# Two gathers at a time: when a graph-attention kernel refills the slots of its ring

## The reference: what is computed

```
h = (x @ W).reshape(n, heads, out_ch)
a_src = sum(h * att_src, -1);  a_dst = sum(h * att_dst, -1)
e = leaky_relu(a_src[src] + a_dst[dst], 0.2)
p = exp(e - segment_max(e, dst)[dst])
alpha = p / segment_sum(p, dst)[dst]
out = segment_sum(h[src] * alpha[..., None], dst)
```

## Time and profile before

| | |
|---|---|
| three runs | 3718.09, 3707.99, 3710.98 us; median 3710.98 us |
| the profiled execution: its own time, its span | 3708.69 us, 3706.9 us |
| busy: PE, DVE, POOL, ACT | 2639.1, 2394.2, 1820.5, 1181.5 us |
| gathers of walk 1, of walk 2 (POOL) | 880 each, 854.8 and 840.7 us busy |
| granted TensorE clock, 300 to 1500 us and 1800 to 3100 us | 0.91 and 0.75 |

### The profile page before, as it was taken

One profiled execution on the slowest core, in us unless ns is written; L12 is line 12 of the kernel. 1 busy time (PEld: TensorE's weight loads), 2 busy tenths in 40 slices (PEclk: granted clock), 3 DMA queues, 4 the chain that ended last, 5 costly groups with the idle time before them and its releaser, 6 DMA issues. The chain is left out here.

```text
span 3706.9 us, 57874 instructions
## 1 busy us (share of the span) xinstructions
PE 2639.1 (71%) x11245; PEld 1963.1 (53%) x11246; DVE 2394.2 (65%) x7306; ACT 1181.5 (32%) x4644; POOL 1820.5 (49%) x1892
## 2 busy tenths in 40 slices
PE   8577777777777777794666666556666666599998
PEld 6455555555555555573455444444444434566666
DVE  6778777777777778884555545555655666635445
ACT  5533433333333333341222111122222211342332
POOL 0365666566656656304555556666655564501111
PEclk9799998889999898997777777777776776599999
DMA  5466666666666666413444563633333333422220
GB/s 192 148 188 187 192 188 193 185 185 189 188 188 185 188 190 184 122 52 114 139 138 135 136 177 106 181 106 106 102 95 95 96 108 103 138 75 64 68 89 12
DMA packets 230811, 511.90 MB, mean 138 GB/s; under 512 B 49249, under 2 KB 116044, under 8 KB 230611
## 3 DMA queue, kind: packets, MB, share of 16 engines
q0 software_dynamic: 118128, 361.70, 34.6%
q1 hardware_dynamic: 97958, 134.64, 12.0%
q10 hardware_dynamic: 14524, 13.40, 1.1%
HBM read 463.94 MB, written 49.57 MB: 139 GB/s over the span
## 5 line engine op out<-in xcount | busy, mean ns | idle before, releaser
L1329 POOL DMA_INDIRECT weights<-table,w_idx x880 | 840.7, 955 | 718.9 <-issue 313.4
L815 POOL DMA_INDIRECT w_G<-table,w_idx x880 | 854.8, 971 | 605.5 <-issue 299.2
L927 PE MATMUL PS<-w_G,w_S 128*128 128x260 f32 x3520 | 954.4, 428 | 90.9 <-DVE ACC L1016 57.7
L927 PEld LDWEIGHTS PS<-w_G,w_S 128*128 128x128 f32 x3520 | 724.1, 212 | 253.8 <-issue 99.9
L1515 PE MATMUL PS<-weights 128*128 128x257 f32 x1760 | 618.9, 497 | 119.3 <-issue 55.5
L1515 PEld LDWEIGHTS PS<-weights 128*128 128x128 f32 x1760 | 398.9, 247 | 227.8 <-issue 135.7
L1004 DVE TENSOR_TENSOR w_G<-w_G,PS 128x512 f32<-128x512 f32 x660 | 432.3, 683 | 68.2 <-ACT PS L838 31.2
L1710 DVE TENSOR_TENSOR ACC<-ACC,PS 128x257 f32 x464 | 196.3, 423 | 412.1 <-remote 185.7
L1016 DVE TENSOR_TENSOR ACC<-ACC,PS 128x520 f32 x464 | 321.0, 692 | 211.4 <-PE PS L927 83.7
L851 ACT ACTIVATE w_G<-w_G 128x64 f32<-128x64 f32 x1760 | 443.8, 334 | 0.2
L1351 ACT ACTIVATE w_PW<-w_Z 128x4 f32<-128x4 f32 x220 | 45.2, 205 | 1077.9 <-DVE w_Z L1695 785.3
(11 more groups left out here) (324 smaller groups left out, 3422.4 us busy)
## 6 DMA issues: line engine op xcount, KB each, us to landing
w_DR<-rows SPq DMA_DIRECT2D x146, 384.0 KB
weights<-in_L_ffn_w SPq DMA_DIRECT2D x16, 1024.0 KB, 7.7
w_G<-table,w_idx POOLq DMA_INDIRECT x880
weights<-table,w_idx POOLq DMA_INDIRECT x880
table<-ACC SPq DMA_DIRECT2D x49, 260.0 KB
xbuf<-XR SPq DMA_DIRECT2D x8, 1040.0 KB
XR<-xbuf SPq DMA_DIRECT2D x7, 1040.0 KB, 5.4
table<-row ACTq DMA_DIRECT2D x49, 129.0 KB, 2.2
```

What stands on the lines that cost most here:

```text
L815: pool.indirect_dma_start(G[:, r, b, :], None, table, IndexOn(ap=idx[:, r, b:b + 1], axis=0)).then_inc(fetched[r], 16)
L927: last = pe.matmul(PS[:, 2 * at + a, 0:W // layer.banks], lhsT, rhs, start=b == slots[0], stop=b == slots[-1])
L1329: pool.indirect_dma_start(G[:, r, b, :], None, table, IndexOn(ap=idx[:, r, b:b + 1], axis=0)).then_inc(fetched[r], 16)
```

## The change

Before, POOL waited once per batch. Now it waits before slots 0 and 1 for the last sum that reads these two, and before slots 2 and 3 for the batch's last sum, and counts `released` up at both places. The new helper gives the number to wait for: for a normal batch the first sum and then the second, for a batch of four sums the second and then the fourth. The same edit is made in both walks. No other engine's list changes.

```diff
+def sums_of_half(b, half):
+    return [k for k, _, slots in steps_of(b) if slots[-1] < 2 * half + 2][-1] + 1
...
             def fetch(n, r, before=None):
                 pool.wait_ge(staged, n + 1)
-                if before is not None:
-                    pool.wait_ge(summed, sums_after(before))
-                pool.sem_inc(released, 1)
                 for b in range(B):
+                    if before is not None and b % 2 == 0:
+                        pool.wait_ge(summed, sums_of_half(before, b // 2))
+                    if b % 2 == 0:
+                        pool.sem_inc(released, 1)
                     pool.indirect_dma_start(G[:, r, b, :], None, table, IndexOn(ap=idx[:, r, b:b + 1], axis=0)).then_inc(fetched[r], 16)
```

## The result

The changed kernel takes 3695.88 us, median of 10 runs (3688.46 to 3704.11), the kernel before 3710.66 us, median of 10 (3700.15 to 3721.66). The ratio is 0.9961, 95% interval 0.9947 to 0.9975. The forecast was 3687 us.

What follows compares the result with a forecast made beforehand. POOL's stretches of gathers were taken to pace both walks. Arrival 0, added instructions 0 and stretch length −17 − 7 = −24 us took 3708.69 to 3684.7; the median's 2.3 us offset gave 3687 us, own range 3640 to 3699, 8-in-10 range 3630 to 3750.

Steps and rivals of the forecast that it cites:

- POOL's stretches pace the walks: Both walks: unbroken gathers back something up, other engines crawl until POOL's stretch drains; 6.38 and 6.50 us per batch.
- Earlier arrival is worth 0: Both walks: first pair asked for about 2 us earlier gains 0, since DVE does not wait for gathers.
- The added instructions are worth 0: POOL's 428 extra waits and counts in the refills: hidden while a gather is issued, 0, at most +20 us.
- The stretch-length term, −24 us: POOL's stretches: 1.68 us each plus 1.355 per gather; fours join longer ones, −24 us, bounds −92 and +80.
- The size in each walk: Stretches of four taken up: 17 us saved in walk 1, a quarter of at most 27 us, 7, in walk 2.
- The rival that nothing moves: Both walks: DVE and PE stall for a reason of their own, POOL waits for them; 3711 us, chance 0.23.
- The rival of the half-batch breaks: Stretches also end before a batch's third gather, each restart costing 1.68 us; +40 us, 3751 us, chance 0.21.
- The rival of the fixed length of eight: POOL can't have more than eight gathers in hand before draining, so finer waits change nothing; 3711 us, chance 0.08.
- DVE's holes ahead of the merges lose the same total: Sign of being right: POOL's pauses fall by a tenth or more, DVE's holes ahead of L1016 lose the same total.
- Pairs start about 2 us sooner: Sign of being right: the first sum's lead shows as pairs starting about 2 us sooner after PE.

Runs made afterwards that it cites:

- shifted pairs: The change, but slots 0 and 1 wait for the batch's last sum, slots 2 and 3 for the next batch's first; against the kernel before, 3672.68 us, ratio 0.9885.
- stretches of eight and sixteen: The kernel before, but POOL waits only at every second batch, for the sums of both, then issues eight gathers: 3746.71 us, ratio 1.0235.
- the change's parts: Against the kernel before, on a chip without pauses: change in walk 1 alone 1.0003, walk 2 alone 0.9991, both waits for the batch's last sum 0.9998.
- stand-in: The kernel before with each refill waiting for the sums of the batch after its own: 3659.27 us, ratio 0.9993; its profile stands for the kernel before.

## Why the prediction was right, and where it was wrong

- *POOL's stretches pace the walks.* Right in the main for the kernel as it was measured: edits of POOL's waits alone move the time by −1.15% to +2.35%, and with half of the gathers the walks shrink to 1169.7 and 1032.4 us. That this goes by the stretches, and not by the number of gathers, rests on the shifted pairs and the stretches of eight and sixteen. It is a property of some chips, which one profile could not show: elsewhere POOL issued 464 gathers in a row, and the change's parts moved nothing.
- *Earlier arrival is worth 0.* Right: a batch later is 0.9993, and the pairs that come one sum later than the change's are the best of all. The transfer's end can be read from the queue's packets: from a gather's start to its last packet it takes 3.4 us in walk 1 and 2.5 in walk 2, in the median, against at least three batches of lead. The Trainium skill's rule ("DMA: Bandwidth & Descriptors", Anatomy of one DMA), by which I estimated 2.6 us for the 266,240 bytes of walk 1, is 0.8 us short there; for the 132,096 bytes of walk 2 it gives an estimated 2.3 us, 0.2 short.
- *The added instructions are worth 0.* Right within the measurement: 1.0011 (0.9994 to 1.0028), which is −2 to +10 us.
- *The stretch-length term, −24 us.* The sum was near (−14.8 us by the medians; −22.4 and +9.2 us by the walks of the two profiles), the step behind it wrong, so that the sum came out near is luck. The step said that stretches of four would be taken up into longer ones, that pauses would become fewer by a tenth, and that each saved 1.68 us. Stretches of four did become fewer (24 to 10, and 62 to 32), and sixes and tens appeared, but the pauses became more, 138 and 141 for 117 and 130. The fault was to read the 1.68 us as the fixed price of a stretch. They came from one stretch of eight of walk 1 and one of twelve of walk 2; by the median pauses of walk 1's own eights and twelves (2.64 and 3.40 us) the same sum gives 0.82. Starting again costs some 0.45. The line described stretches as they were; it did not say that fewer of them would be cheaper. With fewer by construction, the kernel is 2.35% slower.
- *The size in each walk.* Walk 1, −17 us forecast: −22.4 in the first pair of profiles, −36 against the stand-in on the second chip. Walk 2, −7 us forecast: +9.2 and +8. That is about what two profiles of the same walk 2 differ by (8.7 us), but the ratios point the same way: 0.9931 with walk 1 alone, 0.9961 twice with both. Whether the change does harm in walk 2 or only no good is not settled, since the intervals overlap and the chips differ.
- *The rival that nothing moves, because POOL only waits for the others.* Its number falls: 3711 us, against a ratio whose interval (0.9947 to 0.9975) leaves out 1. Its reason is half right. POOL's pauses are for the most part waits for PE and DVE, as it said; but these don't stall for a reason of their own, since with half of POOL's gathers the holes ahead of DVE's merges nearly go in walk 1 and fall to a third in walk 2.
- *The rival of the half-batch breaks.* Its premise came true in full: 78 and 73 pauses stand ahead of a batch's third gather. Its price did not. It charged each break 1.68 us and would have turned the kernel slower from some 85 batches on. Breaks are mostly paid for by shorter pauses: the median after two gathers is 1.62 us in walk 1, after eight 2.45, after ten 2.89. I read this as time that the stretch would have taken from DVE and PE anyway; that is not shown.
- *The rival of the fixed length of eight.* It falls: a finer wait was to change nothing, and in walk 1 the eights went from 89 to 62 and 13 tens appeared (and before there were 19 longer ones, not 18); on a chip without pauses there are stretches of 464. The Trainium skill's queue of 8 for GPSIMD ("Advanced Engine Details and Errata", Engine Queue Depths) is thus no limit on such a stretch, though in the kernel before DVE's and PE's slow steps begin at the seventh or eighth gather in 59 of the 83 stretches of walk 1 that have any.
- *DVE's holes ahead of the merges lose the same total.* Half right: 38 us less in walk 1, 16 more in walk 2.
- *Pairs start about 2 us sooner.* I did not measure this, and the shifted kernel shows that it would not have mattered.

What stays open: what it is that POOL's gathers fill, if anything, and by what it holds up DVE and PE; why it does so on two or three of the chips and not on two others; and whether the shifted pairs gain in walk 2 where the change doesn't (12.6 us between two profiles). The gathers' own packets are not late: in a stretch of walk 1, a gather's last packet lands 2.1 us after its issue ended for the first gather and 2.4 to 2.5 for the third to eighth, and within 0.15 us the same on the chip without pauses. A small added distance between gathers on a chip with pauses wasn't tried.

## What to carry to other kernels

When one engine's pauses line up with the holes of the others, ask who stops whom before giving the pause a price. A regression over stretches as they happen to fall (1.68 us each) is no price list for stretches that you force; one kernel with fewer and longer ones told the two readings apart. Where a long list of gathers slowed everybody, as here on two chips, letting it go in small parts, each tied to the consumer's next step, was worth more (1.15%) than letting it go early.

## What the runs showed of the hardware

- The same kernel took 3153, 3660 and 3711 to 3715 us on different chips, 18% from end to end, at the same issue time of a gather (0.95 us, and 0.30 to the next). Verdicts on such a kernel have to be taken side by side on one chip, and hold for chips of its kind.
- On the slower ones, register arithmetic of 40 ns on DVE takes up to 0.73 us. Of 263 such slow steps in walk 1 before, 162 start while POOL goes on issuing gathers and the rest within 1.7 us after its last. Beside a stretch of sixteen DVE and PE stood for over 10 us, DVE until the count of a sum was recorded that by its modelled end was done 12.6 us before. With half of the gathers, in stretches of two, no such slow step is left in walk 1, and the merges' idle time there is 6.9 us instead of 211.4.
- Behind a wait that stopped POOL, a gather starts 0.75 to 0.8 us after the wait is over, on both kinds of chip and also where POOL waits for its own memset (0.79 us), some 0.45 to 0.5 us more than behind another gather.
